# An attention layer with group norm on one core: the first image's head in another order

## The chip, the core and the metric

The kernel runs on one core of a Trainium2 chip. The metric is the device time of one launch, in microseconds. Before the change three executions took 1976.14, 1978.31 and 1979.01 us: the median is 1978.31.

## What is computed

Sixteen images of 512 channels and 32 x 32 pixels go through a group norm, three 1x1 convolutions, an attention over the 1024 pixels, an output convolution and a residual add, all in float32:

```python
h = group_norm(x, gamma, beta)                 # 32 groups of 16 channels
q, k, v = (conv1x1(h, w, b) for (w, b) in ((wq, bq), (wk, bk), (wv, bv)))
attn = softmax(einsum('bci,bcj->bij', q, k) * 512 ** -0.5, axis=2)
out = x + conv1x1(einsum('bcj,bij->bci', v, attn), wo, bo)
```

## The kernel before

The convolutions are folded. Since q.k = h' (wq' wk) h plus terms of the biases, the kernel forms the 512 x 512 product of wq and wk once ("wkq", banks 0 to 3 of the PSUM) and a vector t_bias = wk' bq; then T = wkq h for each image, and scores = h' T. In the same way wo and wv are folded into one weight "wov" (banks 4 to 7), whose product with h replaces v and the output convolution. wo has to be transposed for that: 16 transposes of 128 x 128 on TensorE.

Each product of full precision is three matmuls in TensorE's fast float32 format (the function `product`): each operand is a high part, which ScalarE casts ("high_..."), and a low part, the difference to the exact value, which VectorE (or GpSimd, for wv) subtracts ("low_..."). A block is usable for TensorE once its low part is there.

The products T, scores and h x wov are each made of seven half-size products instead of eight. Operands are quarters of h (A11, A12, A22) and sums of quarters (S1 = A21 + A22, S3 = A11 - A21, S2 = S1 - A11, S4 = A12 - S2), and quarters of the weights and sums of these (wt 1 to 7). Products are numbered 1 to 7; the table `OF_H` says which h block each reads (4: A22, 5: S1, 2: A12, 7: S3, 6: S2, 1: A11, 3: S4), `T_ORDER` in which order TensorE makes them, `H_FIRST` in which order VectorE makes the low parts of the h blocks in the first image, `W_ORDER` that of the weights. Each product has two rows (r = 0, 1) of 6 matmuls with 512 columns. Between the products of one bank ScalarE copies its content away ("snap": a after product 4, b after 2, y after 6), and VectorE forms the sums D3, D1, D2, B11, B22, B21 (`add_t`, `C_ORDER`), whose high and low parts are the operands of the scores. D4 is read from the bank itself.

There is no scheduler: the five engines' programs are written out, each engine runs its list in order, and semaphores join them. The whole change lies in the head, before and in the first image. There, in order:

- SyncE issues the loads: wk and wq by blocks, bq, x of image 0, wo, the vectors gamma, beta, bo, and wv, all in one queue.
- TensorE (from L428): 12 filler matmuls on a block of zeros, wk x wq (48 matmuls), 16 transposes of wo, the bias product (4 small matmuls into bank 4, two passes each), wov (48 matmuls), then `make_first_t`, `make_scores`, `make_v`, `outputs_0`, `outputs_1`.
- ScalarE: casts of wk, wq; four activations for the bias terms (L664); casts of wo's transposes (L671) and of wv (L674); h normalised by halves (L642, channel blocks 2 and 3 first); seven weight casts (L658); h blocks (L651); `first_parts`.
- VectorE: low parts of wk, wq; statistics of image 0 (L895 to L933); low parts of wo (L989); sums of weights (L995 to L1000); weights' low parts (L1007, L1011); h (L964); `make_first_t` of its own.
- GpSimd: sums of the bias terms (L374, L376), h's scale and shift (L366 to L385), low parts of wv (L361).

In `make_scores` the four score products of group 7 come first (24 matmuls). The next, product 1 of pixel block q = 0, writes the bank that D4 and the B21 sum of row 0 read, so it waits for this sum:

```python
if p == 1:
    if q == 0:
        pe.wait_ge(t_split, t_count(b, first, 7, 0, L_AT[4]))
        pe.wait_ge(t_added, t_count(b, first, 6, 0, C_AT["B21"]))
```

Later images run the same parts in a loop (`images`), with their own orders; the change leaves those as they are.

## Time and profile before

| what | us |
|---|---|
| timed executions | 1976.14, 1978.31, 1979.01 |
| profiled execution | 1976.81, its span 1974.8 |
| TensorE busy (of the span) | 1966.2 |
| VectorE busy | 1630.7 |
| ScalarE busy | 998.1 |
| first matmul of T | starts at 36.38 |
| first matmul of the scores | starts at 55.42 |

The span is the time from the first to the last instruction of the core. A matmul's busy time overlaps that of the next (0.39 us each, started every 0.227 us), so the distance of starts is what counts. Idle time of an engine stands in brackets in a timeline, with what ended it.

### The profile page before, as it was taken

Reading aid. Unit: us, or ns where it says so; the run is one execution under the profiler, and the core shown is the slowest. Engines: PE = TensorE matmul, PEld = TensorE weight load, DVE = VectorE, ACT = ScalarE, POOL = GpSimd, SP = SyncE. Lnnn points to the kernel's source line nnn. Section 1 sums busy time; section 2 is a strip of 40 time slices with the busy share of each in tenths; the row PEclk is TensorE's granted clock in tenths of the full one; section 3 lists DMA queues with packets and bytes.
Section 4 is the critical chain, followed back from the end, with each engine's and each line's share of the span. In section 5 each row is a group of like instructions: output and inputs, shape, how many; then the busy total and the mean of one; then the engine's idle time right before and its main releaser. Section 6 shows DMA issues by size and latency. Waiting matters only on the chain.

```text
span 1974.8 us, 29827 instructions
## 1 busy us (share of the span) xinstructions
PE 1966.2 (100%) x9924; PEld 1680.8 (85%) x9924; DVE 1630.7 (83%) x2285; ACT 998.1 (51%) x1528; POOL 327.0 (17%) x240
## 2 busy tenths in 40 slices
PE   9999999999999999999999999999999999999999
PEld 7888888888888888888888888888888888888887
DVE  8998896978969789696887969889698896978857
ACT  6474453645536464454644536446364553646443
POOL 2022120111202012020121201212011120212202
PEclk9999999999999999999999999999999999999999
DMA  7336252363414535054350533615236252363402
GB/s 250 128 150 171 76 148 96 149 170 127 114 77 155 164 149 139 31 173 146 149 159 32 173 125 149 170 66 151 102 149 170 108 124 87 150 169 149 92 31 43
DMA packets 55035, 254.66 MB, mean 129 GB/s; under 512 B 8160, under 2 KB 8160, under 8 KB 50400
## 3 DMA queue, kind: packets, MB, share of 16 engines
q1 hardware_dynamic: 36720, 221.01, 29.8%
q0 software_dynamic: 18288, 33.30, 10.8%
q8 instruction: 16, 0.26, 0.1%
q14 instruction: 11, 0.09, 0.0%
HBM read 213.39 MB, written 74.45 MB: 146 GB/s over the span
## 4 chain that ended last, share of the span: by engine, by line
PE 94%; DVE 0%; issue 0%; POOL 0%; ACT 0%; POOLq 0%
PE psum L419 32%; PE psum L420 31%; PE psum L421 31%; DVE red L1161 0%; DVE scores L1166 0%; POOL wide L394 0%; DVE scores L1152 0%; DVE scores L1351 0%; DVE scores L1220 0%; ACT room L730 0%; POOLq L393 0%; ACT scores L744 0%
## 5 line engine op out<-in xcount | busy, mean ns | idle before, releaser
L419 PE MATMUL psum<-big_hi 128*128 128x512 f32 x1056 | 412.0, 390 | 1.6 <-POOL big_lo L361 1.6
L420 PE MATMUL psum<-big_lo,big_hi 128*128 128x512 f32 x1056 | 411.6, 390 | 0.0
L421 PE MATMUL psum<-big_hi,big_lo 128*128 128x512 f32 x1056 | 411.4, 390 | 0.0
L419 PE MATMUL psum<-big_hi,h_hi 128*128 128x512 f32 x896 | 348.5, 389 | 0.0
L420 PE MATMUL psum<-big_lo,h_hi 128*128 128x512 f32 x896 | 348.5, 389 | 0.0
L421 PE MATMUL psum<-big_hi,h_lo 128*128 128x512 f32 x896 | 348.5, 389 | 0.0
L1152 DVE TENSOR_TENSOR scores<-psum,room 128x512 f32<-128x512 f32 x192 | 130.6, 689 | 199.6 <-ACT room L826 149.6
L826 ACT COPY room<-psum 128x512 f32<-128x512 f32 x192 | 113.1, 589 | 291.2 <-PE psum L421 291.2
L419 PE MATMUL psum<-w_split,h_hi 128*128 128x256 f32 x896 | 253.6, 283 | 0.3 <-ACT room L730 0.3
L420 PE MATMUL psum<-w_split,h_hi 128*128 128x256 f32 x896 | 253.6, 283 | 0.0
L421 PE MATMUL psum<-w_split,h_lo 128*128 128x256 f32 x896 | 253.6, 283 | 0.0
L419 PEld LDWEIGHTS psum<-big_hi 128*128 128x128 f32 x1056 | 198.8, 188 | 42.6 <-issue 1.7
L421 PEld LDWEIGHTS psum<-big_hi,big_lo 128*128 128x128 f32 x1056 | 198.6, 188 | 41.7
L420 PEld LDWEIGHTS psum<-big_lo,big_hi 128*128 128x128 f32 x1056 | 198.8, 188 | 40.6
L1173 DVE TENSOR_TENSOR big_lo<-scores,big_hi 128x512 fp32r<-128x512 f32 x256 | 197.2, 810 | 24.9 <-ACT big_hi L754 24.9
L420 PEld LDWEIGHTS psum<-big_lo,h_hi 128*128 128x128 f32 x896 | 168.2, 188 | 35.0
L421 PEld LDWEIGHTS psum<-big_hi,h_lo 128*128 128x128 f32 x896 | 168.2, 188 | 34.9
L419 PEld LDWEIGHTS psum<-big_hi,h_hi 128*128 128x128 f32 x896 | 168.2, 188 | 34.9
L394 POOL PARTITION_ALL_REDUCE wide<-red x32 | 56.9, 1828 | 841.2 <-DVE red L1161 841.2
L1166 DVE TENSOR_TENSOR scores<-scores,wide 128x1024 f32<-128x1024 f32 x128 | 162.8, 1322 | 32.8 <-POOL wide L394 32.8
L405 POOL PARTITION_ALL_REDUCE wide<-red x32 | 104.1, 3254 | 478.3 <-DVE red L1201 469.4
L419 PE MATMUL psum<-h_hi,w_split 128*128 128x512 f32 x448 | 174.5, 389 | 0.0
(134 smaller groups left out, 3445.3 us busy)
## 6 DMA issues: line engine op xcount, KB each, us to landing
w_split<-kept_t SPq DMA_DIRECT2D x15, 3584.0 KB, 11.8
w_split<-kept_v SPq DMA_DIRECT2D x15, 3584.0 KB, 11.3
room<-in_x SPq DMA_DIRECT2D x64, 512.0 KB, 3.5
out<-scores POOLq DMA_DIRECT2D x127, 256.0 KB, 6.8
room<-in_x SPq DMA_DIRECT2D x61, 256.0 KB, 5.7
red<-in_x SPq DMA_DIRECT2D x30, 256.0 KB, 3.7
wide<-in_x SPq DMA_DIRECT2D x30, 256.0 KB, 6.9
kept_t<-w_split SPq DMA_DIRECT2D x1, 3584.0 KB, 10.9
```

The source lines that it names most:

```text
L394: nc.gpsimd.partition_all_reduce(wide[:, half, :], red[:, half, :], P, MAX_ALL).then_inc(max_all, 1)
L405: nc.gpsimd.partition_all_reduce(wide[:, half, :], red[:, half, :], P, ADD_ALL).then_inc(sum_all, 1)
L419: nc.tensor.matmul(o, a_hi, b_hi, start=start, stop=False, skip_group_check=True)
L420: nc.tensor.matmul(o, a_hi, b_lo, start=False, stop=False, skip_group_check=True)
L421: return nc.tensor.matmul(o, a_lo, b_hi, start=False, stop=stop, skip_group_check=True)
L826: nc.scalar.copy(snap_s(q, n), bank[alpha_s[q % 2]][:]).then_inc(s_snapped, 1)
L1152: nc.vector.tensor_tensor(scores[:, o, :], bank[at][:], snap_s(q, n), ALU.add).then_inc(s_added, 1)
L1166: nc.vector.tensor_tensor(scores[:, j:j + 2, :], scores[:, j:j + 2, :], wide[:, half, :].unsqueeze(1).to_broadcast([P, 2, HALF]), ALU.subt ...
L1173: nc.vector.tensor_tensor(p_lo[:, j, :], scores[:, half * NJ + j, :], p_hi[:, j, :].bitcast(F32), ALU.subtract).then_inc(p_split, 1)
```

## The change

TensorE gets 8 filler matmuls instead of 12. The bias product moves ahead of the transposes and into bank 7; the last transposes, which write that bank, wait until ScalarE has copied t_bias out. In wov the first block of wv is split by VectorE (new semaphore `wv_first`), the other three by GpSimd; each bank of wov waits only for its own low part of wo. gamma and beta are loaded by ScalarE's queue after the casts of wk and wq, bo after the bias activations. ScalarE casts h's raw quarters A22 and A12 ahead of the weights. T's products stand in the order 4, 2, 5, 7, 6, 1, 3 (`T_FIRST`), each with its own wait for a weight. S1 of the first image lies in another buffer (`red`), and two snapshots change places. VectorE's list of dots with bv, sums and low parts is rearranged.

```diff
+T_FIRST = (4, 2, 5, 7, 6, 1, 3)
+T_FIRST_AT = {p: n + 1 for n, p in enumerate(T_FIRST)}
...
-H_FIRST = (A22, S1, A12, S3, S2, A11, S4)
+H_FIRST = (A22, A12, S1, S3, S2, A11, S4)
...
@@ -281,11 +284,10 @@
                 sp.dma_start(full[:, k, :], x_d[0][:, k, :]).then_inc(x0_in[k], 16)
             for o in range(KC):
                 sp.dma_start(wo_raw[:, o, :], w_d["o"][:, o, :]).then_inc(wo_in[o], 16)
-            for n, a in enumerate(vec_d):
-                sp.dma_start(vecs[:, n, :], a, allow_slow_non_contiguous=True).then_inc(vec_in, 16)
             for o in range(KC):
                 sp.dma_start(wv_raw[:, o, :], w_d["v"][:, o, :]).then_inc(wv_in[o], 16)
-            sp.wait_ge(wv_split, KC)
+            sp.wait_ge(wv_first, 1)
+            sp.wait_ge(wv_split, KC - 1)
             sp.dma_start(bv_rows, bv.partition_broadcast(P)).then_inc(bv_in, 16)
 
...
-            for o in range(KC):
+            for o in range(1, KC):
...
             pe.wait_ge(filler_set, 1)
-            for _ in range(12):
+            for _ in range(8):
                 nc.tensor.matmul(bank[7], h_hi[:, 0, 0, 0:P], h_hi[:, 0, 0, :], start=True, stop=True,
                                  skip_group_check=True)
             for o in range(KC):
@@ -436,26 +438,30 @@
                                  wk_hi[:, o, :], wk_lo[:, o, :], o == 0, o == KC - 1)
                     if o == KC - 1:
                         mm.then_inc(wkq_summed, 1)
+
             pe.wait_ge(consts_set, 4)
+            pe.wait_ge(bias_step, 2)
+            for c in range(KC):
+                mm = nc.tensor.matmul(bank[2 * KC - 1][:, c:c + 1], wide[:, 0, cols(c)], primer[:, 0:1],
+                                      start=True, stop=True, skip_group_check=True)
+            mm.then_inc(bias_summed, 1)
             for c in range(KC):
                 pe.wait_ge(wo_in[c], 16)
             for n in range(KC):
+                if n == KC - 1:
+                    pe.wait_ge(t_bias_set, 1)
                 for c in range(KC):
                     mm = nc.tensor.transpose(bank[KC + n][:, cols(c)], wo_raw[:, c, cols(n)], ident[:])
                 mm.then_inc(wo_turned, 1)
-
-            pe.wait_ge(wot_split, 1)
-            pe.wait_ge(bias_step, 2)
-            for c in range(KC):
-                mm = nc.tensor.matmul(bank[KC][:, c:c + 1], wide[:, 0, cols(c)], primer[:, 0:1],
-                                      start=True, stop=True, skip_group_check=True)
-            mm.then_inc(bias_summed, 1)
             for o in range(KC):
                 if o == 0:
-                    pe.wait_ge(t_bias_set, 1)
-                pe.wait_ge(wot_split, KC if o == 0 else o + 1)
-                pe.wait_ge(wv_split, o + 1)
+                    pe.wait_ge(wv_first, 1)
+                else:
+                    pe.wait_ge(wv_split, o)
                 for c in range(KC):
+                    if o == 0:
+
+                        pe.wait_ge(wot_split, c + 1)
                     mm = product(bank[KC + c], wvs_hi[:, o, cols(c)], wvs_lo[:, o, cols(c)],
                                  wot_hi[:, o, :], wot_lo[:, o, :], o == 0, o == KC - 1)
                     if o == KC - 1:
@@ -471,8 +477,9 @@
 
             def make_first_t():
 
-                pe.wait_ge(wt_split, 7)
-                for p in T_ORDER:
+                pe.wait_ge(wt_split, 3)
+                for p in T_FIRST:
+                    pe.wait_ge(wt_split, W_AT[p])
                     pe.wait_ge(h_split, H_FIRST_AT[OF_H[p]])
...
 
+            for n in range(2):
+                act.dma_start(vecs[:, n, :], vec_d[n], allow_slow_non_contiguous=True).then_inc(scale_in, 16)
 
             act.wait_ge(bq_in, 16)
             for o in range(KC):
                 nc.scalar.activation(bias_terms[o], wk_raw[:, o, :], ACT.Identity,
                                      scale=bq_s[:, o:o + 1]).then_inc(terms_set, 1)
+            act.dma_start(vecs[:, 2, :], vec_d[2], allow_slow_non_contiguous=True).then_inc(vec_in, 16)
             act.wait_ge(wkq_summed, 2)
             act.wait_ge(bias_step, 1)
             nc.scalar.copy(b12_copy, b12).then_inc(b12_copied, 1)
-            for o in range(KC):
+            act.wait_ge(bias_summed, 1)
+            nc.scalar.copy(t_bias[:], bank[2 * KC - 1][:, 0:KC]).then_inc(t_bias_set, 1)
+
+            def high_wot(o):
                 act.wait_ge(wo_turned, o + 1)
                 nc.scalar.copy(wot_hi[:, o, :], bank[KC + o]).then_inc(wot_high, 1)
-            for o in range(KC):
+
+            def high_raw_wv(o):
                 act.wait_ge(wv_in[o], 16)
                 nc.scalar.copy(wvs_hi[:, o, :], wv_raw[:, o, :]).then_inc(wv_high, 1)
-                if o == 0:
-                    act.wait_ge(bias_summed, 1)
-                    nc.scalar.copy(t_bias[:], bank[KC][:, 0:KC]).then_inc(t_bias_set, 1)
+
+            high_wot(0)
+            high_raw_wv(0)
+            for o in range(1, KC):
+                high_wot(o)
+            for o in range(1, KC):
+                high_raw_wv(o)
             for k in (2, 3):
                 normalise(0, k)
+            high_h(0, 0, True)
+            high_h(0, 1, True)
 
             act.wait_ge(wd_set, 4)
             for p in W_ORDER:
                 high_wt(p)
-            high_h(0, 0, True)
             for k in (0, 1):
                 normalise(0, k)
...
             def first_parts():
 
+                for r in range(2):
+                    snap(0, r, 0, "a", T_FIRST_AT[4], True)
                 high_h(0, 2, True)
-                high_h(0, 1, True)
                 copy_wov(0)
                 copy_wov(1)
                 high_h(0, 3, True)
-                for r in range(2):
-                    snap(0, r, 0, "a", T_AT[4], True)
                 high_h(0, 5, True)
                 high_h(0, 4, True)
                 for r in range(2):
-                    snap(0, r, 1, "b", T_AT[2], True)
+                    snap(0, r, 1, "b", T_FIRST_AT[2], True)
                 for r in range(2):
                     high_t(0, r, "D3", True)
                 high_h(0, 6, True)
                 for r in range(2):
...
@@ -988,6 +1006,10 @@
                 dve.wait_ge(wot_high, o + 1)
                 nc.vector.tensor_tensor(wot_lo[:, o, :], bank[KC + o], wot_hi[:, o, :].bitcast(F32),
                                         ALU.subtract).then_inc(wot_split, 1)
+                if o == 0:
+                    dve.wait_ge(wv_high, 1)
+                    nc.vector.tensor_tensor(wvs_lo[:, 0, :], wv_raw[:, 0, :], wvs_hi[:, 0, :].bitcast(F32),
+                                            ALU.subtract).then_inc(wv_first, 1)
 
             dve.wait_ge(wkq_summed, KC)
             dve.wait_ge(wq_split, KC)
@@ -1000,6 +1022,8 @@
             nc.vector.tensor_tensor(neg_d4, b21, d2, ALU.subtract).then_inc(wd_set, 1)
             dve.wait_ge(t_bias_set, 1)
             nc.vector.tensor_tensor(t_step[:], t_bias[:, 2:4], t_bias[:, 0:2], ALU.subtract).then_inc(biases_set, 1)
+            low_h(0, 0, True)
+            low_h(0, 1, True)
             for p in W_ORDER:
 
                 dve.wait_ge(wt_high, max(W_AT[p], 3))
@@ -1010,7 +1034,6 @@
                 else:
                     nc.vector.tensor_tensor(wt_lo[:, p - 1, :, :], wt_from[p], wt_hi[:, p - 1, :, :].bitcast(F32),
                                             ALU.subtract).then_inc(wt_split, 1)
-            low_h(0, 0, True)
 
             dve.wait_ge(wt_split, 7)
...
@@ -1066,35 +1089,42 @@
                                                accum_out=wo_bv[:, c:c + 1]).then_inc(bv_used, 1)
 
             def make_first_t():
-                low_h(0, 1, True)
                 low_h(0, 2, True)
-
-                dve.wait_ge(bv_in, 16)
-                dve.wait_ge(vec_in, 16 * len(vec_d))
-                for c in (0, 1):
-                    row_dots(c)
                 low_h(0, 3, True)
                 sum_h(0, 2, True)
 
+                dve.wait_ge(bv_in, 16)
+                dve.wait_ge(vec_in, 16)
+                row_dots(0)
+                low_h(0, 4, True)
+                low_h(0, 5, True)
+                row_dots(1)
+
                 dve.wait_ge(wov_summed, KC)
                 add_t(0, 0, "D3", True)
-                low_h(0, 4, True)
-                low_h(0, 5, True)
                 sum_h(0, 3, True)
                 add_t(0, 1, "D3", True)
                 for c in (2, 3):
                     row_dots(c)
+                low_h(0, 6, True)
                 dve.wait_ge(bv_used, KC)
                 nc.vector.tensor_tensor(out_bias[:], wo_bv[:], bo_s, ALU.add).then_inc(biases_set, 1)
-                low_h(0, 6, True)
-                low_t(0, 0, "D3", True)
-                low_t(0, 1, "D3", True)
-                for name in C_ORDER[1:]:
-                    for r in range(2):
-                        add_t(0, r, name, True)
-                for name in L_ORDER[1:]:
-                    for r in range(2):
-                        low_t(0, r, name, True)
+
+                def add_both(*names):
+                    for name in names:
+                        for r in range(2):
+                            add_t(0, r, name, True)
+
+                def low_both(*names):
+                    for name in names:
+                        for r in range(2):
+                            low_t(0, r, name, True)
+
+                low_both("D3")
+                add_both("D1", "D2", "B11")
+                low_both("D4", "B11", "D2", "D1")
+                add_both("B22", "B21")
+                low_both("B22", "B21")
 
             def left(b, n):
```

In the parts left out, GpSimd waits for `scale_in` (gamma and beta) instead of `vec_in`, T_AT becomes T_FIRST_AT for the first image, a cast of A12 waits for two normalised blocks only, and S1 is written to `first_blocks`.

TensorE between the last matmul of wk x wq and the first column of wov. Rows with `ident` are the transposes, those with `primer` the bias product. Before:

```order
L421 MATMUL psum<-big_hi,big_lo 128x512
L444 MATMUL psum<-ident,scores 128x128 [waits wo_in2,wo_in1,wo_in3,wo_in0,consts_set]
L444 MATMUL psum<-ident,scores 128x128 x15
L450 MATMUL psum<-primer,wide 128x1 [waits bias_step,wot_split]
L450 MATMUL psum<-primer,wide 128x1 x3
L419 MATMUL psum<-big_hi 128x512 [waits wv_split,wot_split,t_bias_set]
```

After:

```order
L423 MATMUL psum<-big_hi,big_lo 128x512
L445 MATMUL psum<-primer,wide 128x1 [waits bias_step,consts_set]
L445 MATMUL psum<-primer,wide 128x1 x3
L454 MATMUL psum<-ident,scores 128x128 [waits wo_in2,wo_in3,wo_in1,wo_in0]
L454 MATMUL psum<-ident,scores 128x128 x11
L454 MATMUL psum<-ident,scores 128x128 [waits t_bias_set]
L454 MATMUL psum<-ident,scores 128x128 x3
L421 MATMUL psum<-big_hi 128x512 [waits wot_split,wv_first]
L422 MATMUL psum<-big_lo,big_hi 128x512
L423 MATMUL psum<-big_hi,big_lo 128x512
L421 MATMUL psum<-big_hi 128x512 [waits wot_split]
```

The bias product stands ahead of the transposes, which are cut at the twelfth by a wait for t_bias, and the columns of wov wait one by one.

ScalarE behind the casts of wk and wq, up to the h blocks (L658 in both is another function: weight casts before, h blocks after; `vecs` are gamma, beta, bo). Before:

```order
L639 CAST big_hi<-scores 128x512 [waits wq_in3]
L664 ACTIVATE red<-scores,bq_s 128x512 [waits bq_in]
L664 ACTIVATE red<-scores,bq_s 128x512
L664 ACTIVATE wide<-scores,bq_s 128x512 x2
L668 COPY red<-psum 128x512 [waits bias_step,wkq_summed]
L671 CAST big_hi<-psum 128x512 [waits wo_turned] x4
L674 CAST big_hi<-scores 128x512 [waits wv_in0]
L677 COPY t_bias<-psum 128x4 [waits bias_summed]
L674 CAST big_hi<-scores 128x512 [waits wv_in1]
L674 CAST big_hi<-scores 128x512 [waits wv_in2]
L674 CAST big_hi<-scores 128x512 [waits wv_in3]
L642 ACTIVATE room<-room,h_shift,h_scale 128x1024 [waits scale_step] x2
```

After:

```order
L669 DMA vecs<-in_gamma 128x4x1
L669 DMA vecs<-in_beta 128x4x1
L673 ACTIVATE red<-scores,bq_s 128x512 [waits bq_in]
L673 ACTIVATE red<-scores,bq_s 128x512
L673 ACTIVATE wide<-scores,bq_s 128x512 x2
L675 DMA vecs<-in_bo 128x4x1
L678 COPY red<-psum 128x512 [waits bias_step,wkq_summed]
L680 COPY t_bias<-psum 128x4 [waits bias_summed]
L684 CAST big_hi<-psum 128x512 [waits wo_turned]
L688 CAST big_hi<-scores 128x512 [waits wv_in0]
L684 CAST big_hi<-psum 128x512 [waits wo_turned] x3
L688 CAST big_hi<-scores 128x512 [waits wv_in1]
```

Three DMA issues are new, t_bias is copied before the first cast of wo, and one cast of wv stands between the casts of wo.

VectorE at the end of T, from D3's low parts to B21's. Rows that write `scores` are sums, rows that write `big_lo` low parts. Before (L1037 is D1, L1041 D2, L1044 B11, L1046 B22, L1050 B21):

```order
L1057 TENSOR_TENSOR big_lo<-scores,big_hi 128x512 [waits t_high] x2
L1037 TENSOR_TENSOR scores<-psum,scores 128x512 [waits t_snapped,t_summed]
L1037 TENSOR_TENSOR scores<-psum,room 128x512 [waits t_snapped,t_summed]
L1041 SCALAR_TENSOR_TENSOR scores<-psum,t_bias,scores 128x512 [waits t_snapped,t_summed]
L1041 SCALAR_TENSOR_TENSOR scores<-psum,t_bias,room 128x512 [waits t_snapped,t_summed]
L1044 TENSOR_TENSOR scores<-scores 128x512 [waits t_added] x2
L1046 TENSOR_TENSOR scores<-scores 128x512 [waits t_added] x2
L1050 TENSOR_TENSOR scores<-psum,scores 128x512 [waits t_high] x2
L1057 TENSOR_TENSOR big_lo<-psum,big_hi 128x512 [waits t_high] x2
L1057 TENSOR_TENSOR big_lo<-scores,big_hi 128x512 [waits t_high] x10
```

After (L1060 is D1, L1064 D2, L1067 B11, L1069 B22, L1073 B21):

```order
L1080 TENSOR_TENSOR big_lo<-scores,big_hi 128x512 [waits t_high] x2
L1060 TENSOR_TENSOR scores<-psum,scores 128x512 [waits t_snapped,t_summed]
L1060 TENSOR_TENSOR scores<-psum,room 128x512 [waits t_snapped,t_summed]
L1064 SCALAR_TENSOR_TENSOR scores<-psum,t_bias,scores 128x512 [waits t_snapped,t_summed]
L1064 SCALAR_TENSOR_TENSOR scores<-psum,t_bias,room 128x512 [waits t_snapped,t_summed]
L1067 TENSOR_TENSOR scores<-scores 128x512 [waits t_added] x2
L1080 TENSOR_TENSOR big_lo<-psum,big_hi 128x512 [waits t_high] x2
L1080 TENSOR_TENSOR big_lo<-scores,big_hi 128x512 [waits t_high] x6
L1069 TENSOR_TENSOR scores<-scores 128x512 [waits t_added] x2
L1073 TENSOR_TENSOR scores<-psum,scores 128x512 [waits t_high] x2
L1080 TENSOR_TENSOR big_lo<-scores,big_hi 128x512 [waits t_high] x4
```

Eight low parts (D4, B11, D2, D1 of both rows) now stand between the sum B11 and the sums B22 and B21.

## Rows read from the trace of the kernel before

**Rows 1.** The page's first part: busy time, share, instructions.
```profile
PE 1966.2 (100%) x9924; PEld 1680.8 (85%) x9924; DVE 1630.7 (83%) x2285; ACT 998.1 (51%) x1528; POOL 327.0 (17%) x240
```

**Rows 2.** TensorE's waits over the whole span: total, times, longest.
```profile
PE psum L419 <- POOL big_lo L361: 1.6, 1, 1.6
...
PE psum L444 <- DMA scores<-in_wo: 0.9, 1, 0.9
PE psum L419 <- ACT room L730: 0.3, 1, 0.3
```

**Rows 3.** Timeline of TensorE: start, length, line, operation, count, idle before.
```profile
1.58 5.49 PE L429 MATMUL psum<-h_hi 128*128 128x512 f32 x12 [1.58 <-DVE h_hi L967]
6.87 0.62 PE L419 MATMUL psum<-big_hi 128*128 128x512 f32 x1
...
19.06 1.94 PE L444 MATMUL psum<-ident,scores 128*128 128x128 f32 x16 [0.88 <-DMA scores<-in_wo]
21.09 1.05 PE L450 MATMUL psum<-primer,wide 128*128 128x1 f32 x8
23.79 0.47 PE L419 MATMUL psum<-big_hi 128*128 128x512 f32 x1 [1.65 <-POOL big_lo L361]
...
36.38 0.39 PE L419 MATMUL psum<-h_hi,w_split 128*128 128x512 f32 x1
...
55.42 0.39 PE L419 MATMUL psum<-big_hi,h_hi 128*128 128x512 f32 x1
```

**Rows 4.** Stretches: length, TensorE busy (count), granted clock, DMA share, GB/s.
```profile
19.00:21.00 2.00, 1.94 (x16) 1.00 1.01 357
21.00:23.80 2.80, 1.06 (x9) 1.00 0.09 33
...
24.40:27.70 3.30, 3.30 (x10) 0.50 0.02 5
```

**Rows 5.** Timeline of ScalarE in the head.
```profile
19.72 2.05 ACT L671 CAST big_hi<-psum 128x512 fp32r<-128x512 f32 x4 [2.28 <-PE psum L444]
...
23.79 2.38 ACT L642 ACTIVATE room<-room,h_shift,h_scale 128x1024 f32<-128x1024 f32 x2
26.07 1.57 ACT L658 ACTIVATE w_split<-psum 128x512 fp32r<-128x512 f32 x3
...
33.01 1.06 ACT L651 CAST h_hi<-room 128x1024 fp32r<-128x1024 f32 x1
```

**Rows 6.** Timeline of VectorE in the head.
```profile
4.85 0.69 DVE L976 TENSOR_TENSOR big_lo<-scores,big_hi 128x512 fp32r<-128x512 f32 x1
...
20.34 2.48 DVE L989 TENSOR_TENSOR big_lo<-psum,big_hi 128x512 fp32r<-128x512 f32 x4 [0.15 <-ACT big_hi L671]
...
31.88 1.22 DVE L964 TENSOR_TENSOR h_lo<-room,h_hi 128x1024 fp32r<-128x1024 f32 x1
...
37.63 0.68 DVE L1064 CUSTOM_DVE_ANT_0 scores<-scores 128x512 f32<-128x512 f32 x1
...
50.59 0.68 DVE L1037 TENSOR_TENSOR scores<-psum,scores 128x512 f32<-128x512 f32 x1
...
57.18 1.27 DVE L1057 TENSOR_TENSOR big_lo<-psum,big_hi 128x512 fp32r<-128x512 f32 x2
```

**Rows 7.** Timeline of GpSimd in the head.
```profile
15.92 1.29 POOL L376 TENSOR_TENSOR wide<-wide 128x512 f32<-128x512 f32 x1
...
22.37 5.01 POOL L361 TENSOR_TENSOR big_lo<-scores,big_hi 128x512 fp32r<-128x512 f32 x4
```

**Rows 8.** SyncE's DMA issues of gamma and beta: start, length.
```profile
10.25 0.43 SPq L285 DMA_DIRECT2D vecs<-in_gamma  x1
10.73 2.20 SPq L285 DMA_DIRECT2D vecs<-in_beta  x1
```

**Rows 9.** DMA packets of the stretch from 11 to 16 us.
```profile
DMA packets 696, 2.07 MB, mean 415 GB/s; under 512 B 78, under 2 KB 78, under 8 KB 696
```

**Rows 10.** DMA packets of the stretch from 17 to 20 us.
```profile
DMA packets 2013, 0.78 MB, mean 262 GB/s; under 512 B 1633, under 2 KB 1633, under 8 KB 2013
```

28 lines of the change are left out of this document (14 added, 14 removed).

## Prediction

> **What bounds the kernel now.** I read the page's first part, then all waits of TensorE, then its timeline from 0 to 60 us, since only the first image's code is touched, and last the other engines over the same stretch. The first part [rows 1] has TensorE busy for 1966.2 of 1974.8 us: nothing but TensorE's idle time and its clock is to be had. The waits [rows 2] name 2.8 us of idle: 1.6 for GpSimd's low part of wv, 0.9 for the load of wo, and 0.3 after the first scores. Nothing behind 60 us waits but that 0.3, so a microsecond lost or won in the head stays to the end.
>
> TensorE's timeline [rows 3]: filler from 1.58, products of wk and wq from 6.87, a halt from 18.18 to 19.06, transposes of wo, the bias product, a halt to 23.79, the 48 matmuls wv x wo, first T product at 36.38, first scores at 55.42. The clock table [rows 4] shows a granted clock of 1.00 over the transposes, the bias product and the second halt, and 0.50 (the 1.2 GHz level) over 24.4 to 27.7. At 2.4 GHz the pitch of a 512-column matmul is (55.42 - 36.38)/84 = 0.227 us (84 = 7 products x 12), so the 48 need 10.9 us; they took 12.6. The low stretch costs 1.7 us. So the head holds 0.9 + 1.65 + 1.7 us, 4.2 us or 0.21% of the time, beside the filler.
>
> **Fewer fillers (12 to 8).** 12 took 5.49 us with their tail, 0.43 each [rows 3]; 8 end at 5.0. The first low part of wq ends at 5.54 [rows 6], so the first product starts at 5.6 instead of 6.87. Gain of the wk/wq section: up to 1.3 us; at least -0.4 (an idle half microsecond among the fillers could leave the first dozen products at the slow pitch). Either way TensorE then stands before wo, which lands at 19.0 [rows 3]. Worth 0 itself; it makes room for the bias product.
>
> **Bias product into that gap.** It takes 1.05 us [rows 3] and waits for GpSimd's second sum, done at 15.92 + 1.29 = 17.21 [rows 7]. ScalarE's activations for it now stand behind two DMA issues. No DMA is issued by ScalarE in this trace; on SyncE the same two vectors took 0.43 and 2.20 us to issue [rows 8]. With 0.43 each, less 0.3 that ScalarE idles there for bq, the sum comes at 17.8, the product ends at 18.85, and wo decides still. With 2.20 each the sum comes at 21.3 and the transposes, behind it in TensorE's order, at 22.3: +3.3 us. I take 0.43: the 2.20 came behind many loads on SyncE's own queue.
>
> **Where wo lands.** gamma and beta were behind wo on one queue; now they are on another, beside x and wo. Between 17 and 20 us 1633 packets under 512 B went, and the rate was 262 GB/s against 415 between 11 and 16 [rows 9, 10]: (1 - 262/415) x 3 = 1.1 us for 1633, so 0.7 us for the 1024 of gamma and beta. If all pass ahead of wo's last packets the transposes start 0.7 later; if none, 0. I take 0.5. Call the start of the transposes W: 19.06 before, 19.56 after, bounds 19.0 and 22.4.
>
> The Trainium skill, "DMA: Bandwidth & Descriptors", section "Queues, rings and completion order", says that a DMA engine takes turns between its queues packet by packet. By it nearly all small packets meet x and wo, delay 0.7. Its section "Bandwidth" has about 10.5 ns a packet; 64 on each of 16 engines give an estimate of 0.7 us, and the trace agrees with that (0.7).
>
> **From W to the first T product.** Before, wv x wo began at W + 4.73, after four casts and four low parts of wo, the casts of wv, and GpSimd's first low part. Now: first cast of wo ends at W + 1.28 (19.72 + 0.62 before), the cast of wv's first block at W + 1.80, VectorE does the low part of wo (0.60 pitch: 2.48/4) and then that of wv to W + 2.57 [rows 5, 6]. The first product starts at W + 2.6. The other columns' low parts come every 0.6 us, a column takes 3 x 0.227 = 0.68: no wait. GpSimd's blocks (5.01 us for four [rows 7]) end at about W + 5.1, 6.3 and 7.5, needed at W + 5.3, 8.0 and 10.8. So 48 matmuls end at W + 13.5, plus c for the low clock.
>
> c: the halt without large matmuls is from 17.5 or so to 22.2, 4.7 us, where before it was 18.2 to 23.8, 5.6 us. In the trace the clock survived the transposes and fell 6.2 us after the halt began. If it holds, c = 0; if the low stretch recurs on the products, c = 1.7; two such stretches would be 3.4. Nearest is the row: c = 1.7.
>
> T products also need h and weights. ScalarE: casts of wo and wv to W + 4.8, two normalisations (2.38 for two) to 7.1, casts of A22 and A12 (1.07 each, 0.95 pitch) to 9.0, seven weight casts (1.57 for three) to 12.5, two normalisations to 14.8 [rows 5]. VectorE: A22 and A12 low to 10.5, then weights at 0.60; the fourth, which the first product wants, ends at W + 13.0 [rows 6]. Just covered. First T product T0 = W + 13.5 + c = 19.56 + 13.5 + 1.7 = 34.75, against 36.38: 1.6 us early.
>
> **What is late next: VectorE.** Before, T0 came 3.3 us after A22's low part (33.10 [rows 6]); that slack is what is being spent. S1 is the third block in the new order. ScalarE now copies both snapshots of product 4 before it casts S1: product 4 ends at T0 + 2.72 + 0.16, copy 0.5, cast 1.06: S1's low part starts at X = T0 + 4.44 and ends 0.2 to 0.3 after T0 + 5.44, where TensorE wants it. From X, VectorE's order gives (1.14 per 128x1024 instruction, 0.60 per 128x512, 0.66 with a bias, 0.7 per dot with bv [rows 6]): S1 low to 1.1; wait for ScalarE (two copies, cast of S3) to 1.9; S3 low 3.1; sum S2 4.2; dot 4.9; wait for S2's cast to 5.4; S2 low 6.5; A11 low 7.6; dot 8.4; D3 sum 9.0; sum S4 10.2; D3 sum 10.8; two dots 12.3; S4's cast is done at 12.5; S4 low 13.6; bias 13.85; two D3 low 15.05. S4's low part is 1.4 us late for the last T product. The D1 sums start at D = X + 15.05.
>
> Then the new order of sums and low parts. The scores' first product after the four of group 7 writes the bank that the B21 sum of row 0 reads, and waits for it. In between stood 10 sums with 4 low parts behind, 14 instructions, done at 59.6 for a need at 55.42 + 24 x 0.227 = 60.87. Now 8 low parts stand ahead of B22 and B21: 6 sums (3.7), 8 low parts (4.8), two B22 (1.2), B21 (0.7) = 10.4 us. That score product starts at X + 25.5 = T0 + 30.0. It was T0 + 24.5. The 5.5 us more on the T section eat the early start: 34.75 + 30.0 = 64.75 against 60.87, **3.9 us later**. Split: +1.7 with nothing delayed and the clock held, +0.5 for wo, +1.7 for c. If only my count of VectorE were off, each instruction is 0.6 to 1.1 us.
>
> After that VectorE's last low part comes at about D + 13.4, T0 + 33, before ScalarE's c12 copies want it (some 10 us later), and nothing gives the time back [rows 2].
>
> **Base.** The profiled execution took 1976.81 us (span 1974.8, 2.0 around it); the three timed ones 1976.14, 1978.31, 1979.01. The sum is against the profiled one, which is 1.5 below the median; their phases differ by as much as the terms here, so I set the sum on the mean of the four, 1977.6: 1981.5. A difference below 0.2%, 4.0 us, can't be told from none.
>
> **Rivals.**
> 1. The clock holds (c = 0): +2.2, 1979.8. For it: a halt 0.9 us shorter, and 1.00 through the transposes. Against: the halt is nearly as long as before, and its first half now holds even less. Chance 0.24.
> 2. Slower: the head is late. The mechanism is ScalarE's DMA issues taking beta's 2.20 us: one of 0.43 and one of 2.20 bring the bias sum to 19.5 and W to 20.6, 1.0 more than forecast; both bring 2.7 more: 1982.5 to 1984.3. It decides once the sum comes after 18.0. The same size would come from a clock that is low for two stretches, 1983.2. For it: SyncE's rows. Against: ScalarE's own queue is empty. Chance 0.28.
> 3. The early T0 is kept: VectorE's chain isn't late, because ScalarE is earlier than counted or the sums overlap. Then -1.1 (T0 1.6 early, small stalls 0.5) to -3.3 with the clock held: 1974.3 to 1976.5. The order of sums speaks against it; nine instructions would have to vanish. Chance 0.08.
> The forecast itself has 0.40.
>
> **How the numbers follow.** Range 1977.0 to 1985.0: below it the third rival and a lucky base, above it both late issues with a slow base. Slower by over 0.2% (above 1982.3): most of rival 2 (0.22) and a third of the forecast (0.13): 0.35. Faster by over 0.2% (below 1974.4): half of rival 3: 0.04. The rest, 0.61, is within 0.2%. The likeliest's own range is 1979.5 to 1983.5.
>
> **What would show it.** Bias product before the transposes and ended by 19; first transposes at 19.3 to 19.8; wv x wo from 2.6 us behind them; clock 0.50 for some 3 us on it; T0 near 34.7; three small waits of TensorE in T (S1, D3, S4, up to 1.5) and one of about 3.5 us for VectorE's B21 sum ahead of the score product of group 1. Without that long wait the forecast is wrong; with transposes past 20.5, rival 2 is right.

## Result and the profile after

| kernel, same session | median us | lowest to highest | runs |
|---|---|---|---|
| before | 1978.20 | 1975.64 to 1979.82 | 19 |
| after | 1982.09 | 1980.75 to 1983.85 | 19 |

The medians differ by 3.9 us. The ratio of the two kernels is 1.0022 (4.3 us), 95% interval 1.0015 to 1.0028, which is 3.0 to 5.5 us: slower, clear of the noise. The profiled execution of after took 1983.54 us (span 1981.5), 6.7 more than that of before. Each of the two profiles lies some 1.4 us outside its median, on opposite sides, so a part of the 6.7 is chance. A second profile of each kernel (experiments 10 and 11 below) is a better pair.

The first part of the page of after, to be set against [rows 1]:

```profile
PE 1968.0 (99%) x9920; PEld 1680.3 (85%) x9920; DVE 1632.2 (82%) x2286; ACT 1000.1 (50%) x1528; POOL 335.9 (17%) x239
```

TensorE's waits over the span (total, times, longest), against [rows 2]:

```profile
PE psum L421 <- DVE scores L1073: 3.3, 1, 3.3
...
PE psum L421 <- DVE h_lo L982: 1.5, 2, 1.3
PE psum L454 <- DMA scores<-in_wo: 0.9, 1, 0.9
PE psum L421 <- DVE scores L1182: 0.8, 1, 0.8
PE psum L421 <- ACT room L749: 0.6, 1, 0.6
...
PE psum L445 <- POOL wide L378: 0.3, 1, 0.3
```

GpSimd's 1.6 us are gone. In their place stands one wait of 3.3 us for the B21 sum (L1073), and 1.5 for h's low parts. A new one of 0.8 and one of 0.6 (0.3 before) stand in the first image's products with wov. TensorE's timeline shows where, against [rows 3]:

```profile
5.77 0.70 PE L421 MATMUL psum<-big_hi 128*128 128x512 f32 x1 [0.40 <-DVE big_lo L994]
...
17.47 1.02 PE L445 MATMUL psum<-primer,wide 128*128 128x1 f32 x8 [0.31 <-POOL wide L378]
19.37 3.15 PE L454 MATMUL psum<-ident,scores 128*128 128x128 f32 x16 [0.87 <-DMA scores<-in_wo]
22.18 0.78 PE L421 MATMUL psum<-big_hi 128*128 128x512 f32 x1
...
33.73 0.39 PE L421 MATMUL psum<-h_hi,w_split 128*128 128x512 f32 x1
...
39.59 0.47 PE L421 MATMUL psum<-h_hi,w_split 128*128 128x512 f32 x1 [0.26 <-DVE h_lo L982]
...
52.02 0.47 PE L421 MATMUL psum<-h_hi,w_split 128*128 128x512 f32 x1 [1.27 <-DVE h_lo L982]
...
54.84 0.39 PE L421 MATMUL psum<-big_hi,h_hi 128*128 128x512 f32 x1
...
63.73 0.47 PE L421 MATMUL psum<-big_hi,h_hi 128*128 128x512 f32 x1 [3.29 <-DVE scores L1073]
...
64.68 0.63 PE L421 MATMUL psum<-big_hi,h_hi 128*128 128x512 f32 x1
65.11 0.63 PE L422 MATMUL psum<-big_lo,h_hi 128*128 128x512 f32 x1
```

The first product starts 1.1 us earlier, wov 1.6, the first T product 2.65. T is 2.07 us longer (54.84 - 33.73 = 21.11, against 19.04), with waits of 0.26 and 1.27 in it (from start to start they cost 0.5 and 1.5). Group 1 of the scores starts at 63.73, where it was 60.87. From 64.68 on a matmul takes 0.63 us and starts 0.43 behind the last one. That is the 1.2 GHz level, as the clock table shows (columns as in [rows 4]):

```profile
20.00:23.40 3.40, 3.40 (x15) 0.51 0.20 50
...
62.00:64.30 2.30, 0.56 (x3) 1.00 0.00 0
64.30:67.70 3.40, 3.40 (x10) 0.50 0.02 5
67.70:71.00 3.30, 3.30 (x16) 1.00 0.00 0
```

In before these scores ran at 1.00. The head's own low stretch [rows 4: 24.4 to 27.7] now lies at 20.0 to 23.4, two thirds of it over the transposes.

ScalarE's DMA issues, against SyncE's [rows 8], and its list at 62 to 67 us:

```profile
9.28 0.45 ACTq L669 DMA_DIRECT2D vecs<-in_gamma  x1
9.77 0.62 ACTq L669 DMA_DIRECT2D vecs<-in_beta  x1
...
62.42 2.42 ACT L743 CAST big_hi<-scores 128x512 fp32r<-128x512 f32 x4 [4.04 <-DVE scores L1069]
64.75 0.62 ACT L723 CAST w_split<-room 128x512 fp32r<-128x512 f32 x1
...
66.31 0.58 ACT L844 COPY room<-psum 128x512 f32<-128x512 f32 x1
```

VectorE from the D1 sums to the B21 sums, against [rows 6]:

```profile
53.11 0.69 DVE L1060 TENSOR_TENSOR scores<-psum,scores 128x512 f32<-128x512 f32 x1
...
56.89 1.29 DVE L1080 TENSOR_TENSOR big_lo<-psum,big_hi 128x512 fp32r<-128x512 f32 x2
58.09 3.69 DVE L1080 TENSOR_TENSOR big_lo<-scores,big_hi 128x512 fp32r<-128x512 f32 x6
61.70 1.29 DVE L1069 TENSOR_TENSOR scores<-scores 128x512 f32<-128x512 f32 x2
62.90 1.28 DVE L1073 TENSOR_TENSOR scores<-psum,scores 128x512 f32<-128x512 f32 x2
```

Eight low parts (56.89 to 61.7) stand ahead of B22 and B21. ScalarE is idle for 4 us, then casts B22 and B21 and three weights, and only then (66.31) copies score product 1.

### The profile page after: what moved, and what is told of

Its sections match the earlier page's. It is cut to its first block, busy times and chain, and to the rows that moved or that the text cites. A ratio compares the mean times of both kernels' runs of the same rounds, so it can differ in the third digit from the quotient of the medians.

```text
span 1981.5 us, 29819 instructions
## 1 busy us (share of the span) xinstructions
PE 1968.0 (99%) x9920; PEld 1680.3 (85%) x9920; DVE 1632.2 (82%) x2286; ACT 1000.1 (50%) x1528; POOL 335.9 (17%) x239
## 4 chain that ended last, share of the span: by engine, by line
PE 95%; DVE 0%; ACT 0%; issue 0%
PE psum L421 32%; PE psum L422 32%; PE psum L423 32%; DVE red L1191 0%; DVE scores L1182 0%; DVE scores L1381 0%; DVE scores L1250 0%; ACT room L749 0%
```

## The experiments

The table has the start, in us, of the places that the text speaks of: T0 the first T product, S the first score product, G the score product of group 1, V the first product with wov, T1 the T section of the second image. The last column is the distance to the median of before in the same session: 1978.20 for after, 1977.35 for 1 to 4, 1976.95 for 5 to 8, 1977.12 for 9 to 12. Experiments are compared by it; the ratios, with their 95% intervals, stand in the text.

| kernel | transposes | T0 | S | G | V | T1 | V to T1 | median (runs) | to before |
|---|---|---|---|---|---|---|---|---|---|
| before | 19.06 | 36.38 | 55.42 | 60.87 | 93.50 | 157.71 | 64.21 | 1978.20 (19) | 0 |
| before again, exp. 10 | 19.00 | 34.73 | 53.77 | 59.21 | 91.97 | 157.77 | 65.80 | 1976.91 (one) | -0.2 |
| after | 19.37 | 33.73 | 54.84 | 63.73 | 98.09 | 163.73 | 65.64 | 1982.09 (19) | +3.9 |
| after again, exp. 11 | 19.10 | 32.73 | 53.85 | 62.73 | 97.05 | 162.47 | 65.42 | 1981.55 (one) | +4.4 |
| 1 old order of sums | 19.70 | 33.34 | 54.47 | 61.37 | 94.19 | 160.20 | 66.01 | 1977.58 (11) | +0.2 |
| 2 B21 early, B22 late | 18.66 | 32.31 | 53.43 | 59.20 | 98.83 | 164.49 | 65.66 | 1983.47 (6) | +6.1 |
| 3 before, new order | 18.80 | 36.12 | 55.16 | 62.22 | 95.54 | 160.90 | 65.36 | 1978.97 (11) | +1.6 |
| 4 wait filled | 18.86 | 33.34 | 54.42 | 63.33 | 96.64 | 162.42 | 65.78 | 1980.12 (11) | +2.8 |
| 5 as 2, copies first | 20.33 | 34.89 | 56.01 | 61.77 | 97.00 | 162.66 | 65.66 | 1979.93 (11) | +3.0 |
| 6 as 1, vectors on SyncE | 18.67 | 32.31 | 53.43 | 60.34 | 93.11 | 158.83 | 65.72 | 1977.64 (11) | +0.7 |
| 7 as 5, T waits gone | 18.99 | 32.62 | 52.38 | 58.88 | 94.10 | 159.82 | 65.72 | 1978.88 (11) | +1.9 |
| 8 as 1, 12 fillers | 18.93 | 32.56 | 53.68 | 60.58 | 93.35 | 158.64 | 65.29 | 1978.45 (11) | +1.5 |
| 9 as 7, four copies first | 19.59 | 33.28 | 52.98 | 59.48 | 93.38 | 160.32 | 66.94 | 1978.95 (11) | +1.8 |
| 12 as 9, statistics late | 18.70 | 32.34 | 52.11 | 58.61 | 92.67 | 160.04 | 67.37 | 1978.75 (11) | +1.6 |

**1. Only the order of sums and low parts back, all else as after.**

```diff
-                add_both("D1", "D2", "B11")
-                low_both("D4", "B11", "D2", "D1")
-                add_both("B22", "B21")
-                low_both("B22", "B21")
+                add_both("D1", "D2", "B11", "B22", "B21")
+                low_both("D4", "B11", "D2", "D1", "B22", "B21")
```

> The changed kernel with one thing undone: VectorE makes all sums D1, D2, B11, B22, B21 of the first image ahead of the low parts D4, B11, D2, D1, as before. Theory A (the wait for the B21 sum comes from VectorE's late chain plus the 8 low parts in front of it): from the start of D1 at 53.1 us the need of the first group-1 score product (B21 of row 0 and B11's low parts) is 14 instructions x 0.6 = 8.9 us away, 62.0, where TensorE stands since 60.3: the wait shrinks from 3.3 to about 1.7 us, and group 1 starts 1.6 us earlier. If the clock then stays at 2.4 GHz another 1.7 us go. So 1.6 to 3.3 us faster than the changed kernel, 1978.8 to 1980.5. Rival B (the order doesn't matter, the wait ends by something else, or time lost here is given back later): the changed kernel's 1982.1.

1977.58, ratio to before 1.0003 (0.9994 to 1.0012): +0.2 us where after has +3.9, so 3.7 us less, more than the 1.6 to 3.3 expected, and nearly all of the loss.

```profile
61.37 0.50 PE L421 MATMUL psum<-big_hi,h_hi 128*128 128x512 f32 x1 [1.30 <-DVE big_lo L1080]
```

The wait ahead of G is 1.30 instead of 3.29, now for B11's low parts (the last of them is the fourth low part, done at 61.3), and the scores behind it keep their clock (G to V 32.82 against 34.36; before 32.63).

**2. B21's sums early, B22's behind the low parts.**

```diff
-                add_both("D1", "D2", "B11")
+                add_both("D1", "D2", "B11", "B21")
                 low_both("D4", "B11", "D2", "D1")
-                add_both("B22", "B21")
+                add_both("B22")
```

> The changed kernel with the B21 sums moved up behind B11 and the B22 sums behind the low parts of D1: what the first group-1 score product waits for is 12 instructions behind the start of D1. Theory A: ready at 53.1 + 7.5 = 60.6 us, wanted at 60.3: the wait shrinks from 3.3 to 0.3 us, the low stretch of the clock behind it (8 matmuls at 0.43 instead of 0.227 us, 1.7 us) doesn't come, and so the time falls by 3.0 + 1.7 = 4.7 us to about 1977.4, which is the time before or a little less. If the low stretch has nothing to do with the wait: 3.0 us, 1979.1. Rival B: 1982.1.

1983.47, ratio 1.0031 (1.0019 to 1.0044): not faster than after, where 4.7 us less was expected. The long wait is gone ahead of G (0.16 left) and back, longer, 7.4 us behind it. TensorE's wait, then ScalarE's timeline:

```profile
PE psum L423 <- ACT room L846: 4.4, 1, 4.4
```

```profile
62.19 2.26 ACT L745 CAST big_hi<-scores 128x512 fp32r<-128x512 f32 x4 [5.24 <-DVE scores L1071]
64.35 0.61 ACT L725 CAST w_split<-room 128x512 fp32r<-128x512 f32 x1
...
65.91 1.06 ACT L846 COPY room<-psum 128x512 f32<-128x512 f32 x2
```

ScalarE casts B22 and B21 when B22's sums are there (VectorE makes them from 61.47 on), then three weights, and only then copies product 1, which the next score product of that bank waits for: 4.4 us. The late sum can be charged in two places, to TensorE directly and through ScalarE's list; taking the first away only shows the second.

**3. The new order of sums alone, in the kernel before.**

```diff
-                for name in C_ORDER[1:]:
+                for name in ("D1", "D2", "B11"):
                     for r in range(2):
                         add_t(0, r, name, True)
-                for name in L_ORDER[1:]:
+                for name in ("D4", "B11", "D2", "D1"):
+                    for r in range(2):
+                        low_t(0, r, name, True)
+                for name in ("B22", "B21"):
+                    for r in range(2):
+                        add_t(0, r, name, True)
+                for name in ("B22", "B21"):
                     for r in range(2):
                         low_t(0, r, name, True)
```

> The kernel before with one part of the change alone: the new order of sums and low parts at the end of the first T (low parts D4, B11, D2, D1 ahead of the sums B22, B21). Theory A (17 instructions instead of 14 between D1 and the group-1 score product, 10.4 us): ready at 50.6 + 10.4 = 61.0 us against a need at 60.9, so a wait of 0.1 to 0.3 us and the time before, 1978.2, plus 0.3: no difference that can be measured. Rival C (the order is bad by itself, by the 8 low parts, 4.8 us): 3 us and more slower, 1981 or later.

1978.97, ratio 1.0009 (1.0000 to 1.0018): +1.6 us, with a wait of 1.47 ahead of G, where 0.1 to 0.3 was expected. VectorE itself waited 0.67 us in that stretch, for ScalarE's cast of D4 ahead of the second low part, which the count of instructions had left out. The order that costs 3.7 us in after costs 1.6 here: T0 is late (36.12), so VectorE has more slack. The two parts of the change are not additive.

**4. Twelve matmuls inside the long wait, whose result is never read.**

```diff
+                            if first:
+                                pe.wait_ge(t_added, t_count(b, first, 6, 1, C_AT["D2"]))
+                                for _ in range(12):
+                                    nc.tensor.matmul(bank[5], h_hi[:, 0, 0, 0:P], ...)
```

They read the high part of A11 (the buffer that held the zeros of the fillers holds h by now).

> The changed kernel with 12 more matmuls (512 columns, result never read) in TensorE's wait ahead of the first group-1 score product: 12 x 0.227 = 2.7 us of work inside a wait of 3.3. Nothing else moves. Theory D (the wait itself brings the 1.2 GHz stretch behind it, 64.2 to 67.7 us): the granted clock stays 1.00 there and the time falls by 1.7 us to 1980.4. Rival (that stretch comes anyway, or its loss is hidden): 1982.1.

1980.12, ratio 1.0015 (1.0006 to 1.0025): +2.8, 1.1 us less than after (1.7 was expected; the two intervals overlap, so here the profile decides). The scores behind the wait:

```profile
63.30:66.70 3.40, 3.07 (x13) 1.00 0.00 0
```

G starts at 63.33, which is T0 + 29.99 as in after, but the granted clock stays at 1.00 (0.50 in after over the same stretch), and G to V takes 33.31 us instead of 34.36, with a new wait of 0.30 for ScalarE's copy in it. So the wait costs its length and a low stretch behind it.

**5. As 2, with ScalarE's two copies of product 1 ahead of its casts of B22 and B21.**

```diff
-                for name in G_ORDER[1:]:
+                for name in G_ORDER[1:5]:
+                    for r in range(2):
+                        high_t(0, r, name, True)
+                for q in range(2):
+                    act.wait_ge(s_summed, S_AT[1, q])
+                    nc.scalar.copy(snap_s(q, 0), bank[alpha_s[q % 2]][:]).then_inc(s_snapped, 1)
+                for name in G_ORDER[5:]:
                     for r in range(2):
                         high_t(0, r, name, True)
```

> The kernel with B21's sums early (1983.5 us, in which the wait ahead of the first group-1 product shrank to 0.2 us but one of 4.4 us for ScalarE's copy of that product's bank came behind it), with one more edit: ScalarE makes the two copies of product 1 ahead of the casts of B22 and B21 and of the first three weight casts. Theory A2 (the second place that pays for the late B22 sums is ScalarE's list: its copy stands behind four casts that wait for them and three more): the 4.4 us go, and the low clock behind them (6.8 us at 1.2 GHz, 3.4 us lost): 7 us off, about 1976.5 to 1977. Rival B2 (the 4.4 us come from the bank or from TensorE): 1983.

1979.93, ratio 1.0016 (1.0007 to 1.0025): +3.0, 3.1 us less than 2 (7 were expected). The 4.4 became 2.17 us, for the copy of product 6, the next in ScalarE's list. This profile's head was also late (T0 34.89), with a low stretch in it.

**6. As 1, with gamma, beta and bo loaded by SyncE behind wo, as before.**

```diff
-                act.dma_start(vecs[:, n, :], vec_d[n], ...).then_inc(scale_in, 16)
+                sp.dma_start(vecs[:, n, :], vec_d[n], ...).then_inc(scale_in, 16)
```

> The kernel with all sums ahead of the low parts (1977.6 us), with one more thing undone: gamma, beta and bo are loaded by SyncE's queue behind wo, as before, instead of ScalarE's. Theory A (the small packets delay wo when they go beside it): the transposes start 0.3 us earlier (wo was waited for to 19.4 and before to 19.1), and wv lands later, by up to 1 us, which its cast may feel: 1977.3 to 1978. Rival E (the queue of the vectors is worth a microsecond or more through wv's landing): 1978.6 or later, with a wait ahead of wov for wv's casts.

1977.64, ratio 1.0004 (0.9995 to 1.0013), and 1 is at 1.0003. The queue of the vectors is worth nothing that can be measured; the intervals would hide some 1.5 us.

**7. As 5, and the waits in T taken away** (S1 cast between the two snapshots, S4 cast between D3's rows, S4's low part ahead of the last dot).

```diff
-                for r in range(2):
-                    snap(0, r, 0, "a", ...)
+                snap(0, 0, 0, "a", ...)
                 high_h(0, 2, True)
+                snap(0, 1, 0, "a", ...)
...
-                for c in (2, 3):
-                    row_dots(c)
+                row_dots(2)
                 low_h(0, 6, True)
+                row_dots(3)
```

> All mended: B21's sums early, ScalarE's copies of product 1 ahead of the B22 and B21 casts, S1's cast ahead of the second snapshot of product 4, S4's cast ahead of D3's of row 1 and its low part ahead of the last dot. Theory A: the waits of the T section (0.26 and 1.27 us) shrink to under 0.4 together, the one ahead of group 1 stays under 0.8, none behind it: 2 to 3 us less than with all sums first (1977.6), 1974.6 to 1975.6, so 2 to 3 us under the kernel before as well. Rival F (what the head wins is lost in the products with wov, whose waits for sums of the scores grew from 0.25 to 1.8 us as the head became earlier): 1976.5 to 1978.

1978.88, ratio 1.0012 (1.0003 to 1.0021); 1974.6 to 1975.6 was expected. T took 19.76 us and G started at 58.88, the earliest until then and 2 us ahead of before's first profile. At T1 the kernel was 2.1 us behind it: 2.17 for the copy of product 6, and 0.89 + 0.64 in the products with wov, where that profile of before has 0.25. (Other profiles have such waits too; see 10.)

**8. As 1, with 12 fillers.**

```diff
-            for _ in range(8):
+            for _ in range(12):
```

> The kernel with all sums ahead of the low parts (1977.6 us), with 12 fillers instead of 8. Theory A (the wk/wq products end before wo lands either way): they start at 6.9 instead of 5.8 to 6.1 and end at 18.0 instead of 17.2, the bias product ends at 19.1 instead of 18.5, and the transposes start at 19.2 to 19.4: no difference to 0.3 us. Rival G (the 8 fillers are worth their 1.3 us, or the clock falls another way): 0.5 to 1.7 us either way.

1978.45, ratio 1.0009 (1.0000 to 1.0018), against 1.0003 (0.9994 to 1.0012) for 8 fillers: no clear difference. With 12 TensorE still stood before wo for 0.35 us.

**9. As 7, with the copies of products 1 and 6 ahead of the casts and the weight casts behind product 5's copies.**

```diff
+                for n, p in enumerate((1, 6)):
+                    for q in range(2):
+                        act.wait_ge(s_summed, S_AT[p, q])
+                        nc.scalar.copy(snap_s(q, n), bank[alpha_s[q % 2]][:]).then_inc(s_snapped, 1)
...
-                if first:
-                    for n in range(3):
-                        high_wv(n)
...
+                    if first and pair == 0:
+                        for n in range(3):
+                            high_wv(n)
```

> The kernel with everything mended (1978.9 us), in whose profile TensorE still waited 2.2 us for ScalarE's copy of product 6, which stood behind the casts of B22 and B21 and three weight casts: now the copies of products 1 and 6 stand ahead of them, and the weight casts behind those of product 5. Theory A2 (each late sum is paid twice, in TensorE's own wait and in ScalarE's list): the 2.2 us go: 1976.7, 0.5 us or so under the kernel before. Rival F (the products with wov take what the head wins): 1978 or more, with longer waits of TensorE near 98 us.

1978.95, ratio 1.0008 (0.9999 to 1.0017), no different from 7, where 2.2 us less was expected. The 2.17 fell to 0.61, and V came at 93.38. Then:

```profile
95.56 0.36 PE L423 MATMUL psum<-w_split,h_hi 128*128 128x256 f32 x1 [0.60 <-DVE scores L1193]
...
99.25 0.39 PE L423 MATMUL psum<-w_split,h_hi 128*128 128x256 f32 x1 [1.31 <-DVE scores L1193]
```

Two waits for VectorE's sums in the products with wov, 1.9 us (0.89 in 7), took the place of most of what was won. V to T1 is 66.94, the longest until then.

**10. The kernel before once more, one execution.**

> The kernel before once more, for a second profile. If the low stretch of the clock on wov (24.4 to 27.7 us) and the short waits in the products with wov (0.25) are its habit, both are there again; if they are one execution's, the first T product starts up to 1.7 us earlier or the clock falls elsewhere, and the waits behind are 0.5 to 1.2.

1976.91, the time of the first profile (1976.81). But here the head kept its clock in spite of two halts:

```profile
19.00 1.94 PE L444 MATMUL psum<-ident,scores 128*128 128x128 f32 x16 [1.80 <-DMA scores<-in_wo]
21.03 1.05 PE L450 MATMUL psum<-primer,wide 128*128 128x1 f32 x8
```

```profile
21.00:24.00 3.00, 1.33 (x9) 1.00 0.04 16
24.00:28.00 4.00, 4.00 (x19) 1.00 0.01 4
```

T0 came 1.65 us earlier (34.73), V 1.53 earlier, T1 at the same 157.77. VectorE's timeline in front of the products with wov, of this run, of the first profile of before, and of experiment 3:

```profile
76.65 1.44 DVE L895 BATCH_NORM_STATS2 bn<-room 128x6 f32<-128x512 f32 x2
78.74 0.70 DVE L895 BATCH_NORM_STATS2 bn<-red 128x6 f32<-128x512 f32 x1 [0.64 <-DMA red<-in_x]
80.47 0.69 DVE L895 BATCH_NORM_STATS2 bn<-red 128x6 f32<-128x512 f32 x1 [1.04 <-DMA red<-in_x]
81.84 1.34 DVE L895 BATCH_NORM_STATS2 bn<-wide 128x6 f32<-128x512 f32 x2 [0.67 <-DMA wide<-in_x]
83.22 1.23 DVE L1161 TENSOR_TENSOR red<-scores 128x1024 f32<-128x1024 f32 x1
```

```profile
78.19 1.50 DVE L895 BATCH_NORM_STATS2 bn<-room 128x6 f32<-128x512 f32 x2
79.86 0.69 DVE L895 BATCH_NORM_STATS2 bn<-red 128x6 f32<-128x512 f32 x1 [0.16 <-DMA red<-in_x]
80.98 0.69 DVE L895 BATCH_NORM_STATS2 bn<-red 128x6 f32<-128x512 f32 x1 [0.43 <-DMA red<-in_x]
81.78 1.33 DVE L895 BATCH_NORM_STATS2 bn<-wide 128x6 f32<-128x512 f32 x2
83.14 1.23 DVE L1161 TENSOR_TENSOR red<-scores 128x1024 f32<-128x1024 f32 x1
```

```profile
82.63 1.30 DVE L895 BATCH_NORM_STATS2 bn<-red 128x6 f32<-128x512 f32 x2 [0.86 <-DMA red<-in_x]
84.96 1.35 DVE L895 BATCH_NORM_STATS2 bn<-wide 128x6 f32<-128x512 f32 x2 [1.02 <-DMA wide<-in_x]
86.34 1.23 DVE L1167 TENSOR_TENSOR red<-scores 128x1024 f32<-128x1024 f32 x1
```

VectorE takes statistics of image 1 here, which SyncE loads piece by piece, and then the first maximum (L1161, in experiment 3 L1167). In this run the loads were issued 1.54 us earlier (74.07 against 75.61) and the statistics began 1.54 earlier, but VectorE waited 0.64 + 1.04 + 0.67 us for the loads instead of 0.16 + 0.43, and reached the maximum at the same 83.2. Its list from there on, with the sums that TensorE waits for, ran at the same clock times, and TensorE waited 0.98 us for a sum and 0.63 for ScalarE's copy where it had waited 0.25 in all.

One could read this as an early start that is given back. The other profiles say no. These waits of VectorE for the loads come to 1.86 to 2.53 us in thirteen of the fourteen profiles, and to 0.59 in the first of before. That holds where V comes later than there too: in experiment 3 (V 95.54) they are 1.88 us, in after (V 98.09) 2.03. From the issue of the first piece to the maximum it takes 8.62 to 9.33 us in the thirteen, and 7.53 in that one. So the first profile of before is the exception, by 1.1 us or more, whether V is early or late.

**11. The kernel after once more, one execution.**

> The changed kernel once more, for a second profile; the first was taken in one of its slower executions (1983.5 against 1982.1). The waits of 0.26, 1.27 and 3.3 us come again within 0.3, since VectorE's list sets them; the low stretches of the clock (head, and behind the long wait) may lie elsewhere or be fewer, and the time is 1981 to 1983.5.

1981.55. The head kept its clock here too (transposes 19.10, wov 21.73, T0 32.73), the wait ahead of G was 3.27, and the scores behind it ran at the low clock from 62.6 to 66.0.

**12. As 9, with the statistics of image 1 and two maxima behind those sums.**

```diff
-                    if more and pair == 1:
+                    if more and pair == 1 and not first:
                         channel_stats(b + 1)
                         group_variance(b + 1)
...
+                    if late and pair == 1:
+                        channel_stats(b + 1)
+                        group_variance(b + 1)
```

> The kernel with the copies of products 1 and 6 first, and one more edit: in the first image VectorE does the last two pieces and the small operations of image 1's statistics, and two maxima, behind the sums C11 and C21 of the second pair instead of ahead of them. Theory F2 (TensorE's waits of 0.8 to 1.2 and 0.6 us in the products with wov are for C21 sums and the copies behind them, late by VectorE's own list): both waits go, 1.3 us less than the kernel without this edit: 1975.4. Rival H (the waits are given back later by the maxima and the statistics): no difference between the two.

1978.75, ratio 1.0007 (0.9998 to 1.0016), no different from 9, where 1975.4 was expected. The waits for the sums went. One of 1.87 us for ScalarE's copy came, with a low clock behind it; in ScalarE's list this copy stands behind an activation that had waited 2.53 us for VectorE (L1207). Timeline, then windows:

```profile
106.21 0.39 PE L423 MATMUL psum<-w_split,h_hi 128*128 128x256 f32 x1 [1.87 <-ACT room L751]
```

```profile
107.30:110.70 3.40, 3.40 (x19) 0.52 0.00 0
```

None of the kernels beats before; 1, 6, 9 and 12 can't be told from it (their intervals hold 1).

## Why the prediction was right, and where only its sum was

Experiments 10 and 11 compare the kernels with the same clock in the head. Differences of after against before, from the table:

| section | us |
|---|---|
| to T0 | 32.73 - 34.73 = -2.00 |
| T | 21.12 - 19.04 = +2.08 |
| S to G, the wait of 3.27 | 8.88 - 5.44 = +3.44 |
| G to V, low clock behind the wait | 34.32 - 32.76 = +1.56 |
| V to T1 | 65.42 - 65.80 = -0.38 |
| sum at T1 | +4.70; the two times differ by 4.64, the medians by 3.9 |

- **VectorE's chain: right, to 0.2 us.** Forecast G = T0 + 30.0; measured 30.00 in both profiles, and T0 + 24.5 before. The parts: D1's sums at T0 + 19.5 = 53.2 (53.11), B21's wait about 3.5 (3.29, 3.27), S1 0.2 to 0.3 late (0.26), S4 1.4 late (1.27). A small wait at D3, also named, did not come. Experiment 1 shows that the order of sums is the cause: with it undone nearly the whole loss goes.
- **The head's start: right.** The transposes started at 19.37 (forecast 19.56), the bias product ended at 18.49 (18.85), ScalarE issued gamma and beta in 0.45 and 0.62 us (0.43 each), and wov began 2.81 and 2.63 us behind the first transpose (2.6). wo's delay by the small packets (0.5 forecast, 0 to 0.7 the bounds): in the five profiles in which wo ends the halt and ScalarE loads the vectors, the transposes start at 18.86, 18.93, 19.10, 19.37 and 20.33, in the four with SyncE at 18.67, 18.80, 19.00 and 19.06. The medians differ by 0.2. In the other five (1, 2, 7, 9, 12) wo was there first: the transposes began as the bias product ended, at 18.66 to 19.70, so "wo decides still" held in six of eleven heads.
- **c, the low clock in the head: mis-sized.** 48 matmuls ended at W + 13.5 + c. In eight profiles with after's head the clock held and T0 - W was 13.63 to 13.69: c = 0.1 to 0.2. In three (after, 4, 5) it fell and T0 - W was 14.36 to 14.56: c = 0.9 to 1.1. I had 1.7 from before's profile, where the stretch lay wholly on large matmuls [rows 4]; here two thirds lay over transposes. And 1.7 was not a constant of before either: in experiment 10 T0 - W was 15.73 instead of 17.32.
- **The clock behind the long wait: not foreseen, +1.6 to +1.7.** This is the term that the sum put at nothing. I charged the wait its length alone. Experiment 4 takes 1.05 of it back, 1.35 without its new wait.
- **"A microsecond lost or won in the head stays to the end": borne out, but the base was a lucky profile.** From V to T1 eleven profiles take 65.29 to 66.01 us, though V lies anywhere from 91.97 to 98.83 in them (9 and 12, with other lists, take 66.94 and 67.37); what the execution takes behind T1 is 1819.0 to 1819.3 us in thirteen of fourteen (1819.8 in the first of after). Nothing is given back there, and nothing is taken. But [rows 2], with only 0.3 us of waits behind 60 us, came from the one profile in which image 1's loads were quick and V to T1 took 64.21. Its slow clock in the head (T0 1.65 us late) and its quick loads cancelled, which is why 1976.81 and 1976.91 agree. Experiments 1, 6 to 9 and 12 have T0 1.4 to 2.4 us ahead of experiment 10's and T1 0.9 to 2.6 behind it. They lose this before V, and 9 and 12 also behind it: experiment 6 loses 2.08 in T and 1.47 ahead of G, and nothing from G to T1.
- **The second payer: not foreseen.** ScalarE's copy of product 1 stood behind the casts of B22 and B21. It stayed hidden as long as TensorE waited for B21 itself (experiment 2).

So the total (+3.9 forecast on the mean of four executions, +3.9 measured on medians) is nearer than its parts deserve, by luck: c and wo were too high by 1 to 2 us, and the clock behind the wait was left out at 1.7. That 4.0 us "can't be told from none" was too careful: with 19 executions of each kernel 3.9 can.

Of the rivals, the first (the clock in the head holds, 1979.8) had its condition met in experiment 11, but the time was 1981.55, since the low stretch came behind G instead. The second (late DMA issues or two low stretches) fell with 0.45 and 0.62 us; a second low stretch did come in the first profile of after, elsewhere, and that profile (1983.54) lies in its range. The third (the early T0 is kept) fell: -2.00 is followed by +2.08 in T alone.

The Trainium skill, "DMA: Bandwidth & Descriptors", section "Queues, rings and completion order", was weighed in the prediction: by taking turns between the queues wo would have lost 0.7 us. Measured are 0.2 us between the medians of four and five profiles that spread by 0.4 and 1.5, and the five leave out those in which wo came too early to be waited for. This doesn't settle the rule, but its price isn't seen here.

What stays open: why the clock fell in the head in five profiles (both kernels, before in one of two) and held in nine, and why image 1's loads were quicker in one profile. What the other edits are worth one by one is not shown, only their sum: experiment 6 has T0 2.42 us ahead of experiment 10's, and has lost that and 1.1 us more at G.

## What to carry to other kernels

When a stage is made to start earlier, count for each engine the instructions between that start and the first thing that TensorE will want, and follow them also through the in-order list of a third engine: what hides behind the first wait is the next wait. Compare the time between fixed places of the kernel over several profiles before you read a difference into a pair. Against the first profile of before alone, every change here seems to lose some 1.1 us or more between V and T1; against the other profiles only 9 and 12 do. In this kernel a wait of 3.3 us on TensorE was to be charged once for its length and once more, with 1.6 to 1.7 us, for the low clock behind it.
